# Two layers of attention and feed-forward on one core: a block of GpSimd work moved by one unit, five VectorE operations moved ahead of a decoding

## The reference

```
gamma = mean(abs(w)); q = clip(round(w / (gamma + 1e-8)), -1, 1)
```

## Time and profile before

| | |
|---|---|
| median of 3 runs | 822.33 us (822.27 to 823.15) |
| profiled execution | 822.45 us, its span 820.6 us |
| mean granted clock of TensorE | 0.973 |
| TensorE busy | 736.5 us, 90% |
| VectorE busy | 621.0 us, 76% |
| ScalarE busy | 475.4 us, 58% |
| GpSimd busy | 425.8 us, 52% |

### The profile page before, as it was taken

How to read it: one execution, slowest core, us unless ns; L and a number is a source line. 1 busy time by engine, 2 the same in 40 slices (tenths; PEclk the granted TensorE clock), 3 DMA queues, 4 the chain that set the end, 5 groups by cost and what they waited for, 6 DMA issues and landing times. The chain is left out here.

```text
span 820.6 us, 15118 instructions
## 1 busy us (share of the span) xinstructions
PE 736.5 (90%) x5554; PEld 633.6 (77%) x5554; DVE 621.0 (76%) x1103; ACT 475.4 (58%) x778; POOL 425.8 (52%) x369
## 2 busy tenths in 40 slices
PE   3368899999999999999999999999979899999873
PEld 3257788888888888888888888888857777777773
DVE  5989777787687776767768777767347798989965
ACT  4346656655665675665566566657686656565310
POOL 1444364353346558757534433544645495674732
PEclk9999899999999999999999999999979999999985
DMA  5111121112011110111100000021110000000000
GB/s 155 29 40 40 40 79 41 38 44 60 2 24 32 34 47 22 44 32 40 36 2 22 21 2 22 2 54 47 59 35 1 2 1 26 1 1 27 1 26 26
DMA packets 22110, 25.77 MB, mean 31 GB/s; under 512 B 4499, under 2 KB 17171, under 8 KB 22037
## 3 DMA queue, kind: packets, MB, share of 16 engines
q1 hardware_dynamic: 22036, 24.80, 10.6%
HBM read 14.69 MB, written 3.28 MB: 22 GB/s over the span
## 5 line engine op out<-in xcount | busy, mean ns | idle before, releaser
L479 ACT ACTIVATE probs<-t_pair 128x1024 f32<-128x1024 f32 x128 | 131.2, 1025 | 134.0 <-PE t_pair L896 133.8
L659 DVE TENSOR_REDUCE neg_max<-s_pair 128x4 f32<-128x1024 f32 x127 | 155.0, 1220 | 69.3 <-PE s_pair L871 69.1
L371 POOL TENSOR_TENSOR hid<-g,hid 128x512 f32<-128x512 f32 x64 | 82.2, 1285 | 178.6 <-DVE g L770 147.0
L365 POOL TENSOR_TENSOR hid_lo<-hid,hid_hi 128x512 fp32r<-128x512 f32 x64 | 85.3, 1333 | 77.0 <-ACT hid_hi L502 76.9
L871 PE MATMUL s_pair<-K,Q 96*128 96x256 f32 x508 | 85.8, 293 | 12.5 <-DVE neg_max L659 7.7
L871 PEld LDWEIGHTS s_pair<-K,Q 96*128 96x128 f32 x508 | 76.4, 196 | 21.0 <-issue 7.0
L896 PE MATMUL t_pair<-Q,K 104*128 104x512 f32 x256 | 86.0, 417 | 0.2 <-DMA Q<-max_parts 0.2
L938 PE MATMUL down<-hi,hid_hi 128*128 128x256 f32 x256 | 84.3, 329 | 0.8 <-POOL hid_lo L365 0.8
L911 PE MATMUL misc<-probs,V 128*32 128x256 f32 x1024 | 69.0, 387 | 4.0 <-DVE kc L615 3.3
L938 PE MATMUL down<-lo,hid_hi 128*128 128x256 f32 x256 | 72.0, 281 | 0.0
L938 PE MATMUL down<-hi,hid_lo 128*128 128x256 f32 x256 | 71.7, 280 | 0.0
(11 more groups left out here) (260 smaller groups left out, 1934.5 us busy)
## 6 DMA issues: line engine op xcount, KB each, us to landing
stage<-in_ternary SPq DMA_DIRECT2D x18, 256.0 KB, 2.9
Q<-q_hi SPq DMA_DIRECT2D x64, 64.0 KB, 2.0
stage<-in_scales SPq DMA_DIRECT2D x8, 384.0 KB, 3.4
X<-in_x SPq DMA_DIRECT2D x8, 256.0 KB, 4.2
Q<-q_lo SPq DMA_DIRECT2D x32, 64.0 KB, 2.0
Q<-max_parts SPq DMA_DIRECT2D x128, 4.0 KB
out<-X SPq DMA_DIRECT2D x8, 256.0 KB, 2.1
signs<-w_stage SPq DMA_DIRECT2D x9, 128.0 KB, 1.8
```

What stands on the lines that cost most here:

```text
L365: pool.tensor_tensor(hid_lo[:, m % 2, :, :].rearrange("p a n -> p (a n)"), hid[:, m % 2, :], hid_hi[:, m % 2, :, :].rearrange("p a n -> p ...
L371: pool.tensor_tensor(hid[:, m % 2, :], g[:, m % 2, :], hid[:, m % 2, :], ALU.mult).then_inc(S["hid_done"], 1)
L479: act.activation(probs[:, u % 2, th, :], t_pair[:], ACT.Exp, scale=SCALE).then_inc(S["probs_done"], 1)
L659: dve.tensor_reduce(neg_max[:, u % 2, 4 * jp:4 * jp + 4], score_banks(u, jp)[:].rearrange("p (s n) -> p s n", n=SEQ), AX_X, ALU.max, negat ...
```

## The change

`SIGN_AT` goes from 22 to 23. In VectorE's queue all of `nibble_bits(1, k)` for k = 0 to 3 stands in unit -1 in front of `decode(2)`; its former two places are empty. No operation is added or removed.

```
-SUM_AT, GAMMA_AT, SIGN_AT = 10, 21, 22
+SUM_AT, GAMMA_AT, SIGN_AT = 10, 21, 23
...
-                if u == 0:
-                    nibble_bits(1, 2)
-                    nibble_bits(1, 3)
                 if 0 <= u < PAIRS_N - 2:
                     decode(2 * u + 4)
...
                 if u == -1:
+                    for k in range(4):
+                        nibble_bits(1, k)
                     decode(2)
                     decode(3)
                     memory_weights()
                     for kind, n in at[u]:
                         step(kind, n)
                     weights_low(1)
-                    nibble_bits(1, 0)
-                    nibble_bits(1, 1)
```

## The result

| | before | after |
|---|---|---|
| median | 822.3 us (6 runs, 821.15 to 823.15) | 813.99 us (6 runs, 812.33 to 816.0) |
| ratio | | 0.9897, 95% interval 0.9883 to 0.991 |
| profiled execution | 822.45 us, span 820.6 | 812.5 us, span 810.7 |
| last square of the gate (L505) starts | 591.30 | 585.76 |
| from there to the end of the span | 229.30 | 224.94 |

The kernel is 8.3 us faster. 817.3 us was forecast, with a range that ends at 815.0: the direction was right, the size was not. The last two lines say where to look: layer 0, all of the change, gives 5.54 us in the two profiled executions; the other 4.36 us lie behind it, in layer 1, of which no line was changed. The profiled execution after (812.5 us) is the second shortest of its six, so its share behind layer 0 is above the typical one: by the medians it is 8.3 - 5.5 = 2.8 us.

What follows compares the result with a forecast made beforehand. The prediction took VectorE's queue to pace the start and TensorE to be nearly always busy from unit 6, with signs blocks delaying it. Sum: -2.0 (start) - 3.6 + 0.6 (signs) = -5.0 us, 817.3 us, range 815.0 to 820.0.

Steps and rivals of the forecast that it cites:

- The start: Nibble bits moved in front of decode(2): VectorE's five operations take 4.49 us for 6.93; gain taken as 2.0 us.
- The 0.4 us taken off for a late GpSimd subtraction: At the start, decode(4) up to 0.3 us late behind GpSimd's subtraction, plus moved engine meetings: 0.4 us off the 2.4 gain.
- The bound of 2.9 us: Upper bound of the start's gain, if the rest of that stretch runs without any meeting of the engines as well.
- The signs: Signs blocks one unit later, none left in units 29 and 37: gain 2 x 1.80 = 3.6 us.
- The 0.6 us for the new meetings in units 24, 32 and 40: Signs block behind the next batch's mask and rstd makes hid late: 0.2 us for each of three units.
- the rival of 820.3: Three new meetings cost about 1.2 us each, L631 slowed 2.5 times and hid late by as much; chance 0.12.
- The wait for the store in the block: Units 28 and 36: the block's second operation waits up to 0.6 us for the piece's store, 1.2 us free behind; counted 0.
- the last sentence of the sum: Behind unit 40 nothing waits for anything outside the chain, so the forecast's 5.0 us saved stays saved.
- a chance in the start: Rival: the start gives 2.9 us and part of TensorE's slow stretches there goes as well; 815.8 us, chance 0.12.

Runs made afterwards that it cites:

- e3: The changed kernel once more, with nothing altered: median 814.6 us, ratio 0.9918 to the kernel before.
- e9: The changed kernel with eight more copies of one TensorE product in unit 51 (5.7 us added): median 822.33 us, ratio 0.9998 to the kernel before.
- e11: The kernel before with four more copies of one TensorE product in unit 51 (2.9 us added): median 823.05 us, ratio 1.0014 to the kernel before.
- e1: The changed kernel with SIGN_AT back at 22, so only the nibble bits moved: median 819.48 us, ratio 0.9968 to the kernel before.
- e2: The kernel before with only SIGN_AT = 23, nibble bits as before: median 817.92 us, ratio 0.9955 to the kernel before.
- e4: The changed kernel with 40 extra TensorE products in the idle time before its last transposes: median 816.41 us, ratio 0.993 to the kernel before.
- e13: The changed kernel with 54 extra TensorE products in front of its last transposes: median 813.16 us, ratio 0.9897 to the kernel before.
- e8: The kernel before with its first load held back some 2.5 us by ten small GpSimd operations: median 824.58 us, ratio 1.002 to the kernel before.
- e12: The kernel before with eight more copies of one TensorE product in unit 51 (5.7 us added): median 827.01 us.

## Why the prediction was right and wrong

- **The start: the mechanism held, the size was 2.0 for 2.4 to 2.7.** VectorE's queue got shorter by what was worked out (6.93 - 4.43 = 2.5 us). The 0.4 us taken off for a late GpSimd subtraction didn't come: I had carried its slowed time (2.11 us) along, but away from VectorE's operations it takes 1.82, and its neighbour L334 0.72 instead of 0.92. Between units 5 and 9 0.78 us are lost again, by what is not shown; both traces have 6.8 us of half clock between 92 and 104 us, before in two stretches, after in one. Over the nine traces with this part and an undelayed start unit 9 comes at 128.91 to 130.03 us for 131.00, in five of them 1.9 to 2.1 us earlier. That this is the 2.0 of the forecast is luck: the queue gave more, and the loss behind it is not the one that was taken off. The bound of 2.9 us had no working; the most that was seen is e3's unit 1, 2.94 us earlier (48.43 for 51.37).
- **The signs: the gain was right, the price was not.** 3.61 us was forecast and came. The 0.6 us for the new meetings in units 24, 32 and 40 was too careful: 0. The first signs operation took 1.62 us for 1.57, VectorE's L589 took 1.10 us there, where before it took 1.69, with 0.49 us of waiting in front of it and GpSimd's two-input hid_lo beside it. L631 took 0.67 to 0.69 us in all its eight places: the rival of 820.3 fell. The Trainium skill (GPSIMD Engine Reference, section 1, Specifications) names contention with VectorE instructions that have two SBUF inputs and makes no condition on GpSimd's operation. For this case that is too wide: L631 has two SBUF inputs, met a one-input operation of GpSimd in unit 40 and was not slowed (0.68 us). The wait for the store in the block was there twice, 0.4 us each, and hidden, as worked out.
- **The step that failed** is the last sentence of the sum: "Behind unit 40 nothing waits for anything outside the chain, so what is saved stays saved." I took a shift in layer 0 to go through layer 1 one for one. It doesn't: layer 1 takes 224.7 to 229.3 us with the same work (13 traces, those without extra products in it), by the clock that TensorE is granted behind its gaps. In all thirteen the stretch from the transposes behind the first output products to the last transposes is 21.90 to 21.92 us, while the part before the 2.2 us gap's end takes 186.4 to 187.6, the one with the output products 6.2 to 8.7, and the end 10.2 to 11.2. That the shift changed which of these comes most often is what e9 and e11 speak for. By the profiled executions it is 5.5 us in layer 0, inside the forecast's own range, and 4.4 behind it; by the medians 5.5 and 2.8. I had listed the clock only as a chance in the start. Its row for the end stood in the page (the last digit of PEclk, 5) and was not read.
- **A smaller part that I missed** is that a removed stall also removes the clock's fall behind it: 1.5 us more in 4 of 14 places. In the three traces of the kernel before it happened at none. My estimate from the count is 2 x 4/14 x 1.5 = 0.9 us on average, the lesser part of the 2.8 us; which of the untraced executions had it is not known.
- The Trainium skill (TensorE: Matmul & The Clock Gate, Part 1) describes what watches TensorE's activity for the clock as free-running: it isn't reset when a kernel starts. No run here shows it itself. What the runs show fits: the changed kernel's own six times spread over 3.7 us, and its two traces have 224.94 and 227.14 us behind the last square.
- **What stays open:** what decides in a single execution which level the end gets, and how much of the 2.8 us is the place of layer 1 and how much the rest. e9 puts the place at most of it (822.33 for an expected 820.0). e1 and e2 together give 7.3 us in the medians where layer 0 gives 5.5, but their intervals are some 1.4 us to either side each, so they don't decide it.

## What to carry to other kernels

Where a shared loop is paced by VectorE's queue, move the operations that are slowed beside GpSimd's two-input work (L696 0.96 us for 2.44) to where GpSimd is idle. Where another engine's block stands in front of something that TensorE waits for soon, look for a place one unit on: here that gave 3.6 us with the block unchanged. Before forecasting that a saved microsecond stays saved, look for the places where TensorE's granted clock is under 1 behind gaps: there a shift can give or take a good part of what the edit does (here 2.8 us beside 5.5). Measure such an edit by medians of many runs, and compare the time of the unchanged stage in the two traces before crediting the edit with it.

## What the runs showed of the hardware that was not expected

- The same instructions of layer 1 took 224.7 to 229.3 us. In the last 45 to 49 us of it the granted clock was 0.83 in two short traces and 0.76 in two long ones; the first twelve output products took 5.4 us at 1.2 GHz (781.21 to 786.61) and 3.3 at 2.4 (774.34 to 777.64).
- Behind one and the same wait of 1.5 us the clock stayed in 10 of 14 places and fell in 4, with TensorE busy before it; behind the 3.76 us of e4 it fell, behind 0.58 and 0.99 us of e13 it did not.
- In three of the seventeen traces (e8, e9, e12) TensorE had 1.2 GHz from about 16 or 18 us to between 50 and 56 us. In e9 that cost only about 1.2 us up to unit 1 (49.85 for 48.69); VectorE paces that stretch.
